# Edge convolution from split operands in a fused two-layer image and text kernel, with the unit order of the first layer rewritten

## What is computed

```python
gray = einsum('bchw,c->bhw', x, (0.2989, 0.587, 0.114))
edges = conv2d(gray, scharr, padding='SAME')       # 2 output channels, 3x3
edge = sqrt(edges ** 2).sum(axis=1) / 2            # |e0| + |e1|, halved
h = concat([edge, text_embedding(x_txt)], axis=1)  # 8 x 384 x 256
h = h + attn0(layernorm(h)); h = h + ternary_ffn(layernorm(h))
h = h + attn1(layernorm(h)); h = h + moe(layernorm(h))
```

## Time and profile before

| | us |
|---|---|
| median of 3 runs | 1999.88 |
| lowest and highest run | 1999.59, 2004.97 |
| profiled execution, its own time | 1996.78 |
| span of the profiled execution | 1995.0 |

### The profile page before, as it was taken

One profiled execution on the slowest core, in us unless ns is written; L12 is line 12 of the kernel. 1 busy time (PEld: TensorE's weight loads), 2 busy tenths in 40 slices (PEclk: granted clock), 3 DMA queues, 4 the chain that ended last, 5 costly groups with the idle time before them and its releaser, 6 DMA issues.

```text
span 1995.0 us, 35526 instructions
## 1 busy us (share of the span) xinstructions
PE 1768.5 (89%) x10970; PEld 1408.1 (71%) x10970; DVE 1237.8 (62%) x4024; ACT 957.3 (48%) x2645; POOL 552.9 (28%) x784
## 2 busy tenths in 40 slices
PE   3457999999999899899999999992499999999997
PEld 2244676767677686667777777771389998999896
DVE  7446686767777676756677776657754454445442
ACT  2025474666657566565666666640033343333331
POOL 2233324242423411211111111001333335434431
PEclk9668999999999999999999999995589999999998
DMA  6100101101010100102100110002212222222210
GB/s 193 56 27 17 51 2 58 35 24 56 3 43 0 56 26 8 33 1 58 33 32 32 32 32 0 24 25 81 73 48 98 81 75 66 77 72 67 61 38 20
DMA packets 74577, 90.44 MB, mean 45 GB/s; under 512 B 16539, under 2 KB 64710, under 8 KB 74472
## 3 DMA queue, kind: packets, MB, share of 16 engines
q1 hardware_dynamic: 65000, 72.49, 11.1%
q0 software_dynamic: 9472, 16.77, 3.0%
HBM read 71.26 MB, written 25.26 MB: 48 GB/s over the span
## 4 chain that ended last, share of the span: by engine, by line
PE 71%; issue 11%; DVE 8%; POOL 3%; ACT 2%; DVEq 2%; DMA 1%; POOLq 1%; SPq 1%; ACTq 0%
PE bank L1035 17%; PE bank L1539 16%; PE bank L1554 9%; PE bank L983 6%; PE bank L967 5%; PE bank L1018 5%; PE bank L1177 2%; PE bank L906 2%; PE bank L994 1%; PE bank L1057 1%; DVE probs L2177 1%; PE bank L891 1%; DVE at_least L2735 1%; PE bank L907 1%; POOL rstd_a L2946 1%
## 5 line engine op out<-in xcount | busy, mean ns | idle before, releaser
L1660 ACT ACTIVATE probs<-probs,nmax 128x128 f32<-128x128 f32 (+2 forms) x768 | 381.0, 501 | 75.3 <-DVE nmax L2177 75.1
L983 PE MATMUL bank<-cst,probs 128*128 128x128 f32 x1536 | 234.5, 279 | 19.4 <-ACT probsT L1668 11.6
L983 PEld LDWEIGHTS bank<-cst,probs 128*128 128x128 f32 x1536 | 182.4, 143 | 68.4 <-issue 25.8
L1539 PE MATMUL bank<-xeT,gate_w 128*128 128x480 f32 x768 | 189.3, 382 | 1.4 <-issue 1.4
L1539 PE MATMUL bank<-xeT,up_w 128*128 128x480 f32 x768 | 188.2, 380 | 0.0
L2272 DVE COPY probsT<-bank 128x384 f32<-128x384 f32 x256 | 141.4, 552 | 74.0 <-PE bank L983 72.4
L1554 PE MATMUL bank<-down_w,hT 128*120 128x256 f32 x1536 | 182.8, 281 | 0.0
L1554 PEld LDWEIGHTS bank<-down_w,hT 128*120 128x120 f32 x1536 | 181.5, 182 | 0.1
L2988 POOL COPY rinv<-rowsum 128x384 f32<-128x384 f32 x80 | 40.7, 509 | 497.3 <-DVE o1T L2199 294.5
L2882 DVE TENSOR_TENSOR prod<-bank,sil 128x480 f32<-128x480 f32 x128 | 83.8, 657 | 150.5 <-PE bank L1539 150.3
L1668 ACT COPY probsT<-bank 128x384 f32<-128x384 f32 x256 | 121.8, 476 | 113.1 <-PE bank L983 104.4
(11 more groups left out here) (314 smaller groups left out, 3325.1 us busy)
## 6 DMA issues: line engine op xcount, KB each, us to landing
gate_raw<-in_L_ffn_gate_w SPq DMA_DIRECT2D x8, 1024.0 KB, 4.8
up_raw<-in_L_ffn_up_w SPq DMA_DIRECT2D x8, 1024.0 KB, 6.9
down_raw<-in_L_ffn_down_w SPq DMA_DIRECT2D x8, 1024.0 KB, 5.7
img<-in_x SPq DMA_DIRECT2D x8, 768.0 KB, 5.1
residual_rows<-x SPq DMA_DIRECT2D x8, 384.0 KB, 2.5
residual_rows<-h_in SPq DMA_DIRECT2D x8, 384.0 KB, 3.8
xr<-residual_rows SPq DMA_DIRECT2D x8, 384.0 KB, 4.8
hr<-residual_rows SPq DMA_DIRECT2D x8, 384.0 KB, 3.7
```

Source lines behind the costliest of these rows:

```text
L983: last = tr(ps[bank][:, P * q:P * (q + 1)], probs[:, n % 4, SEG[t] + P * j:SEG[t] + P * (j + 1)], ident)
L1539: last = mm(ps[bank][:, 0:HALF], w[:, wp, c, P * m:P * (m + 1)], xeT[:, xp, c, HALF * hf:HALF * (hf + 1)], start=(c == 0 and k == 0), stop ...
L1660: last = f(p, p, ACT.Exp, bias=nmax[:, n % 4, t:t + 1], scale=-1.0, accum_out=rowsum[:, where, t:t + 1])
```

## The change

The filter bands and the gray image are each split into an upper part in the format F32R and a lower part, the rest. For each filter k the bank `conv{k}` now holds both image halves (512 columns), and nine F32R products (three shifts, times upper band with upper gray, upper band with lower gray, lower band with upper gray) and one halo product of 18 rows fill it. The upper gray part is made on ACT (`gray_uppers`), the lower one on DVE (`gray_lowers`); the halo goes by six transfers, each with three overlapping windows of 256 columns, into 18 rows, and ACT puts them into F32R, once for each half with a factor of 1 or 0 for each row (`halo_halves`). ACT writes the first filter's absolute values straight into `h_in` and the second's back into PSUM, and DVE adds them. The setup gets the splits of the weights and four more small loads ahead of `shift_c`.

```diff
...
+gray_hi, gray_lo = gray_parts[:, 0], gray_parts[:, 1]
...
@@ -413,15 +422,16 @@
...
-band = sb("band", [P, 2, 3, P])
-edge_w = sb("edge_w", [3, 2, 2, P])
+band_start = offsets["top"]
+band = sb("band", [P, 2, 2, 3, P], F32R)
+(band_f,), _ = region(band_start + 4 * 6 * P, ("band_f", [P, 2, 3, P], F32))
+edge_w = sb("edge_w", [18, 2, P], F32R)
...
@@ -636,11 +651,15 @@
     def load_halo(i):
-        sp.wait_ge(gray_ready, i + 1)
-        for k, row in enumerate((P - 1, 0)):
-            for dx in range(3):
-                sp.dma_start(halo_gray[dx:dx + 1, k, :], gray[row:row + 1, k, dx:dx + IMG]) \
-                    .then_inc(halo_loaded, 16)
+        sp.wait_ge(gray_split, i + 1)
+        if i > 0:
+            sp.wait_ge(halo_ready, i)
+        for hf, row in enumerate((0, P - 1)):
+            for part in range(3):
+                q = 9 * hf + 3 * part
+                src = gray_parts[row:row + 1, part % 2, 1 - hf, 0:IMG].bitcast(F32)
+                windows = bass.AP(src.tensor, src.offset, [src.ap[0], [1, 3], [1, IMG]])
+                sp.dma_start(halo_rows[q:q + 3, :], windows).then_inc(halo_loaded, 16)
     for s in range(2):
         sp.dma_start(tok[:, s, 1:], a["x_txt"]).then_inc(tokens_loaded, 16)
@@ -656,9 +675,9 @@
         (scharr_b[:].rearrange("p k a b -> p (k a b)"),
          a["L0_tok_scharr"].rearrange("k o a b -> (k o a b)").partition_broadcast(P)),
         (txt_scale, a["L0_txt_scale"].partition_broadcast(P)),
-        (scharr_h[:, 0, :], a["L0_tok_scharr"][0, 0].rearrange("a b -> b a")),
-        (scharr_h[:, 1, :], a["L0_tok_scharr"][1, 0].rearrange("a b -> b a")),
-        (shift_c[:], const[:, COLS["shift"][0]:COLS["shift"][1]]),
+        *[(scharr_h[3 * q:3 * q + 3, 0, :],
+           a["L0_tok_scharr"][:, 0, 2 - q // 3 * 2, :].rearrange("k b -> b k")) for q in range(6)],
+        (shift_c[:], const[:, COLS["shift"][0]:COLS["halo"][1]]),
         (wqkv[:], a["L0_attn_Wqkv"].rearrange("(c p) n -> p c n", p=P)),
         (w1[:], a["L0_attn_W1"].rearrange("(c p) n -> p c n", p=P)),
         (w2[:], a["L0_attn_W2"].rearrange("(m p) n -> p m n", p=P)),
@@ -798,12 +817,12 @@
             load_second()
             load_x()
             load_text_rows()
+            load_image_ahead()
+            load_residual()
             load_halo_rows()
-            load_residual()
-            load_image_ahead()
             spill_x()
+            spill_h()
             store_rows()
-            spill_h()
         else:
             load_x()
             load_residual()
@@ -892,20 +911,19 @@
                 if t == NT - 1:
                     last.then_inc(filled[bank], 1)
-    def convolve(sec, i, img_no, halves):
-        pe.wait_ge(gray_ready, at(img_no, 1, 1))
-        pe.wait_ge(halo_loaded, at(img_no, 96, 96))
-        for hf in halves:
-            name = f"conv{hf}"
+    def convolve(sec, i, img_no, kinds):
+        pe.wait_ge(gray_split, at(img_no, 1, 1))
+        pe.wait_ge(halo_ready, at(img_no, 1, 1))
+        for k in kinds:
+            name = f"conv{k}"
             bank = banks.bank(sec, name)
             banks.wait_free(pe, sec, name, i)
-            for k in range(2):
-                o = ps[bank][:, IMG * k:IMG * (k + 1)]
-                for dx in range(3):
-                    mm(o, band[:, k, dx, :], gray[:, hf, dx:dx + IMG], start=(dx == 0), stop=False)
-                last = mm(o, edge_w[:, hf, k, :], halo_gray[:, 1 - hf, :], start=False, stop=True)
-            last.then_inc(filled[bank], 1)
+            for dx in range(3):
+                for w, x in ((0, gray_hi), (0, gray_lo), (1, gray_hi)):
+                    mm(ps[bank][:], band[:, w, k, dx, :], x[:, :, dx:dx + IMG],
+                       start=(dx == 0 and w == 0 and x is gray_hi), stop=False)
+            mm(ps[bank][:], edge_w[:, k, :], halo[:], start=False, stop=True).then_inc(filled[bank], 1)
     pe.wait_ge(first_loaded, 16 * FIRST_LOADS)
@@ -1631,14 +1649,28 @@
         nc.scalar.copy(q0T[:, 4 * hh:4 * hh + 4, P * t:P * (t + 1)],
                        ps[bank][:].rearrange("p (q n) -> p q n", q=4)).then_inc(freed[bank], 1)
-    def edges(sec, i, img_no, hf):
-        banks.wait_filled(act, sec, f"conv{hf}", i)
-        if img_no[0] is not None or img_no[1] > 0:
-            act.wait_ge(var_ready[LN_FIRST], at(img_no, NT, hf - NT + 1))
-        f(edge[:, hf, :], ps[banks.bank(sec, f"conv{hf}")][:], ACT.Abs) \
-            .then_inc(freed[banks.bank(sec, f"conv{hf}")], 1)
+    def halo_halves(img_no):
+        act.wait_ge(halo_loaded, at(img_no, 16 * HALO_LOADS, 16 * HALO_LOADS))
+        for hf in range(2):
+            last = f(halo[:, hf, :], halo_rows[:], ACT.Identity, bias=0.0, scale=halo_side[:, hf:hf + 1])
+        last.then_inc(halo_ready, 1)
+    def gray_uppers(img_no):
+        act.wait_ge(gray_ready, at(img_no, 1, 1))
+        nc.scalar.copy(gray_hi[:, :, 1:IMG + 1], gray[:, :, 1:IMG + 1]).then_inc(gray_upper, 1)
+    def edges(sec, i, img_no, kinds=range(2)):
+        for k in kinds:
+            banks.wait_filled(act, sec, f"conv{k}", i)
+            bank = banks.bank(sec, f"conv{k}")
+            if k == 0:
+                if img_no[0] is not None or img_no[1] > 0:
+                    act.wait_ge(spilled, at(img_no, 32, 0))
+                f(h_in[:, 0:2, :].rearrange("p t d -> p (t d)"), ps[bank][:], ACT.Abs).then_inc(freed[bank], 1)
+            else:
+                f(ps[bank][:], ps[bank][:], ACT.Abs).then_inc(edge_ready, 1)
     def divisors_of(sec, i, name, layer, u, c):
         act.wait_ge(freed[5], out_index(layer, u, c, take0[5]))
@@ -1872,11 +1914,13 @@
             relu_of(6)
             relu_of(7)
-    for hf in range(2):
-        edges(SETUP, 0, (None, 0), hf)
+    gray_uppers((None, 0))
+    halo_halves((None, 0))
+    edges(SETUP, 0, (None, 0))
     ln_affine(PRO, 0, "lnA0", xTa[:, 0, :], 0, 2)
-    for hf in range(2):
-        edges(PRO, 0, (None, 1), hf)
+    gray_uppers((None, 1))
+    halo_halves((None, 1))
+    edges(PRO, 0, (None, 1))
     for hh in range(2):
         stack_upper_half((None, 0), hh, PRO, 0)
         for t in range(NT):
@@ -2060,19 +2105,33 @@
     ts(scharr_b[:], scharr_b[:], 0.5, None, ALU.mult)
     then()
-    shift = shift_c[:].rearrange("p (y m) -> p y m", y=3)
+    shift = shift_c[:, 0:3 * P].rearrange("p (y m) -> p y m", y=3)
     for y_ in range(3):
         for k in range(2):
             for dx in range(3):
                 w = scharr_b[:, k, y_, dx:dx + 1]
                 if y_ == 0:
-                    ts(band[:, k, dx, :], shift[:, 0, :], w, None, ALU.mult)
+                    ts(band_f[:, k, dx, :], shift[:, 0, :], w, None, ALU.mult)
                 else:
-                    stt(band[:, k, dx, :], shift[:, y_, :], w, band[:, k, dx, :], ALU.mult, ALU.add)
+                    stt(band_f[:, k, dx, :], shift[:, y_, :], w, band_f[:, k, dx, :], ALU.mult, ALU.add)
         then()
-    for k in range(2):
-        ts(edge_w[:, 0, k, P - 1:P], scharr_h[:, k, 2:3], 0.5, None, ALU.mult)
-        ts(edge_w[:, 1, k, 0:1], scharr_h[:, k, 0:1], 0.5, None, ALU.mult)
+    v.tensor_copy(band[:, 0], band_f[:])
+    halo_c = shift_c[0:18, 3 * P:3 * P + 3]
+    ts(scharr_h[:, 1, :], scharr_h[:, 0, :], 0.5, None, ALU.mult)
+    then()
+    v.tensor_copy(edge_hi[:], scharr_h[:, 1, :])
+    tt(band[:, 1], band_f[:], band[:, 0].bitcast(F32), ALU.subtract)
+    then()
+    stt(scharr_h[:, 2, :], edge_hi[:].bitcast(F32), halo_c[:, 2:3], scharr_h[:, 1, :], ALU.mult, ALU.add)
+    then()
+    v.tensor_copy(halo_side, halo_c[:, 0:2])
+    ts(edge_f[:, :, P - 1], scharr_h[:, 2, :], halo_c[:, 0:1], None, ALU.mult)
+    ts(edge_f[:, :, 0], scharr_h[:, 2, :], halo_c[:, 1:2], None, ALU.mult)
+    then()
+    v.tensor_copy(edge_w[:], edge_f[:])
+    sides = slice(0, IMG + 2, IMG + 1)
+    for z in (gray_hi, gray_lo):
+        v.tensor_copy(z[:, :, sides], small[:, 34:36].unsqueeze(1).to_broadcast([P, 2, 2]))
@@ -2119,26 +2178,33 @@
         else:
             ts(dst, k[:, 0:S], cols[:, g:g + 1], cols[:, b:b + 1], ALU.mult, ALU.add).then_inc(f_, 1)
-    def edges(sec, i, img_no, hf):
-        banks.wait_taken(dve, sec, f"conv{hf}", i)
-        if img_no[0] is not None or img_no[1] > 0:
-            dve.wait_ge(spilled, at(img_no, 32, 0))
-        tt(h_in[:, hf, :], edge[:, hf, 0:IMG], edge[:, hf, IMG:2 * IMG], ALU.add)
+    def edges(sec, i, img_no, halves=range(2)):
+        dve.wait_ge(edge_ready, at(img_no, 1, 1))
+        k, f_ = bank_of(sec, "conv1", i)
+        for hf in halves:
+            last = tt(h_in[:, hf, :], h_in[:, hf, :], k[:, IMG * hf:IMG * (hf + 1)], ALU.add)
+        if 1 in halves:
+            last.then_inc(f_, 1)
     def gray_image(c):
         dve.wait_ge(img_loaded, at(c, 16, 16))
         if c[0] is not None or c[1] > 0:
-            dve.wait_ge(halo_loaded, at(c, 96, 0))
+            dve.wait_ge(halo_loaded, at(c, 16 * HALO_LOADS, 0))
         inner = gray[:, :, 1:IMG + 1]
         ts(inner, img[:, 0], GRAY[0], None, ALU.mult)
         then()
```

(13 more changed lines are left out.)

389 lines of the change are left out of this document (207 added, 182 removed).

## The result

The changed kernel took 2051.62 us (median of 4 runs, 2042.91 to 2053.28) against 2000.91 for the kernel before on the same chip (4 runs): 1.024 times as long, 95% interval 1.0208 to 1.0274. It is slower by 2.4%, where I had forecast 1987.0, faster. The profiled execution took 2053.28 us with a span of 2051.4, 56.4 more than before.

The account below looks back on a forecast made before the run. TensorE's own work was taken to bound units 1 to 5, and dependence chains unit 0. Terms -13 (iterations), -5.5 (unit 0), -1 (units 6 and 7), +7 (setup, prologue) gave -12.5 from 1999.88: 1987 us, range 1972 to 1999.

Parts of the forecast that it names:

- The products: Convolution on TensorE: 20 F32R products of 512 columns at 0.254 to 0.302 us each, saving 3.2 us an image.
- the fourth rival: F32R convolution products stream at full rate, 0.215 us each; six units gain 0.8 us each, 1982.6 in all; chance 0.05.
- The start of an iteration: Loop's turn: `divisors_last` waits 1.7 us instead of 2.81, gaining 1.1; a new wait of 1.5 follows at `values(1)`.
- The same gap of DVE stands at each of the loop's turns, so I take it as belonging to the turn, and it stays.: Turn of the first loop: DVE's idle 3.02 us before `invert_last` remains after the change.
- The wait for the divisors' copy: Start of an iteration: TensorE waits 1.5 us at `values(1)`, since ACT's gray copy precedes its copy of the divisors.
- I find no wait in the following part: Iteration up to `norm_mlp`, by DVE's and ACT's lists: no further wait after the 0.2 us at `values(2)` and `queries_keys(0)`.
- What the other engines get: ACT gets 1.3 us more on 54.9, DVE a lower part of 0.74; both lie under TensorE's 81 us of work.
- The prediction had -2.6: One iteration of the first loop: 3.2 + 1.1 - 1.5 - 0.2 = 2.6 us gained, five iterations 13.
- Setup and prologue: Ahead of the first stack products: setup +3.2 us (1 to 6), prologue +3.8, both together +7.
- Unit 0: First unit: POOL's third rotation 5 us earlier and 0.5 from elsewhere, -5.5 us, between 0 and -10.
- Units 6 and 7: Units with changed lists and unchanged work: part of a wait ahead of `norm_mlp` goes, -1 us, from +2 to -4.
- The signs that it had named: Forecast wrong if TensorE waits ahead of the halo product, convolution instructions exceed 0.3 us, or the prologue costs over 10.

Follow-up runs that it names:

- the pair of runs in one order: Changed kernel, third attention normalization moved back, VectorE loops not refetched each turn: new convolution (gray copy behind divisors' copy) 1986.2 us; old convolution and setup 1996.97.
- The placed kernel before: Kernel before with empty VectorE instructions at the head, so that neither VectorE loop is transferred anew at each turn: 1989.5 us.
- only the code is placed: Changed kernel with nothing but 67 empty instructions at VectorE's head, so that neither loop is transferred anew at each turn: 2009.02 us, ratio 1.0039.
- the two placed kernels: Kernel before (1989.5 us) and changed kernel with normalization back and gray copy behind divisors' copy (1986.2), both with VectorE loops not transferred anew each turn.
- the gray image later: Against the changed kernel repaired and placed: VectorE's gray image behind its first value rows, ScalarE's gray copy behind its third exponential group: 1997.09 us, ratio 0.9969.
- repaired and placed: Changed kernel, third attention normalization moved back, gray copy behind divisors' copy, VectorE loops shifted so neither is transferred anew each turn: 1986.2 us, ratio 0.9915.
- 1985.4: Changed kernel, third attention normalization moved back, 67 empty VectorE instructions so neither loop is refetched each turn, gray copy still ahead of divisors' copy: 1985.41 us, ratio 0.9918.
- 51 together: Changed kernel with normalization moved back, gray copy behind divisors' copy and 110 empty VectorE instructions: 2000.24 us, ratio 0.9985; alone 2019.1, 2037.2, 2035.5.

## Why the prediction was wrong

**The products: right.** Forecast 3.2 us less an image, 2.9 by the trace (5.47 for 8.3) and 2.94 by the pair of runs in one order. Nine products of 512 columns in 2.37 us are 0.263 each, inside the range that I took from the rows of 256 and 384 columns; the fourth rival, 0.215, did not come. (The section that it was taken from, the Trainium skill, TensorE: Matmul & The Clock Gate, Back-to-back issue gap, gives this rule for a single product by itself, and for a sustained stream of products of 512 columns a lower figure, 131 ns; the F32R products here took 0.263 us, more than either.)

**The start of an iteration: the step that failed is "The same gap of DVE stands at each of the loop's turns, so I take it as belonging to the turn, and it stays."** It belongs to where VectorE's code lies. The placed kernel before has no such wait and is 11.5 us faster. In the changed kernel the gap was 3.58 instead of 3.02, TensorE waited 2.18 us where 1.7 was forecast, and the clock fell at these waits, which I had not priced at all: of the 95.6 us of an iteration 7.0 go when only the code is placed (88.6). In the kernel before, where the clock held, the gap cost 88.6 - 85.6 = 3.0. The wait for the divisors' copy, 1.5 forecast and 1.16 measured, was right, and most of it belonged to the same cause (0.49 is left when only the code is placed).

**"I find no wait in the following part": wrong.** The added lists were right for what DVE and ACT do and left out POOL. At the end of the iteration stood 2.81 us of wait and 1.6 to 3.4 of lost clock; 4.4 in sum where it stands by itself. The step "What the other engines get" did not ask what POOL does at that time, though `attn_norm(2)` was moved in the diff and releases it. The Trainium skill, SBUF — State Buffer, section Who interferes with whom, says that a VectorE instruction with two SBUF inputs, or a cast in a two-port mode, waits for the whole length of a GpSimd instruction that holds the pair of ports they share. The trace agrees: 1.95 and 1.96 us beside additions of 1.83 and 2.12, each ending 0.2 to 0.4 us behind the addition that it overlaps. It agrees in what was not slowed too: in the kernel before the first of the same additions lay beside masks and a copy that read from PSUM, and these kept their 0.55 us. The kernel before had one normalization of 1.92 us beside another of POOL's additions, so that the trace at hand could have given the warning.

**The second layer: not in the prediction.** +17.3 us by 18 instructions of displacement, more than the prediction's whole sum of -12.5. That all eight units and everything after them could move with a static position was no term and no rival.

**An iteration, put together** from the runs: -2.94 products, +1.6 the order, +4.4 POOL beside DVE, +4.0 the turn (7.0 for 3.0) = +7.1, and the trace has 95.6 - 88.6 = +7.0. The prediction had -2.6. Each term is the difference of two runs in a chain from the kernel before to the changed one, so that the sum must come out; that it does is no proof of the terms. What each stands for rests on the waits and stretches in those runs.

**Setup and prologue: right in the sum, not in the parts.** +7 forecast, +8.9 measured up to the first stack product; between the two placed kernels it is 6.2 (125.95 and 119.73). Start-up differs by up to 6 us among runs of one convolution (113.73, 115.14 and 120.17 with the old one), so that the agreement proves little. The setup cost 1.6 us where 3.2 was forecast (ACT's last absolute value ends at 78.65 for 77.01): its products start 6.8 us later, where 6.3 was forecast, but take 6.95 us and not 8.6. The prologue cost 7.3 where 3.8 was forecast: its products start at 110.16 for 106.4 (1.6 of this comes from the setup) and take 9.3, above the 5.1 to 8.6 of the forecast. At the low clock, twice 5.1 = 10.2, as the prediction itself has it for the setup, was the right bound. Its mean clock of 0.61 for the setup's products is that of 61 to 75 us, which begins before them; over the products themselves it was 0.69.

**Unit 0: mechanism right, result wrong.** POOL's last rotation comes 51.2 us after the first stack product instead of 55.4, 4.2 earlier where 5 was forecast, but the unit ends 2.5 later instead of 5.5 earlier. With 64 us at half clock it took 102.2 and 102.3 in two of the experiments, with 76 to 79 us 106.3 to 106.7 in the changed kernel and six of the experiments, with 86 us 109.9 in one (the gray image later), and before the change 103.9. What brings the clock down there I did not separate.

**Units 6 and 7:** -2.8, forecast -1.

**The signs that it had named did not come.** TensorE did not wait for the halo, a product took 0.26 us in the loop and not over 0.3, and setup and prologue together cost less than 10. All three looked at the convolution, and the loss lay in what stands around it.

**What stays open:** whether the change, repaired and placed, beats the kernel before placed as well. The ratios of 1986.2 and 1985.4 and that of 1989.5 have overlapping intervals. Side by side on one chip, four runs of 1984.64 to 1987.53 stand against five of 1987.19 to 1990.78: 3.3 us less by the medians, 0.2%, which speaks for a small gain and does not settle it. The loop gains 8.1 us in the profiled executions (420.8 for 428.8), and setup and prologue take 6.2 back. What decides whether the clock falls at a wait, and for how long, is open too. Why the new order's transposes are busy for 1.3 us more was not tried.

## What to carry to other kernels

Before a change to the length of a program with loops is priced, look at the queue of instruction transfers and at idle time put down to "issue" at each turn: if a loop shows them, try the same kernel with a few dozen empty instructions at its head before anything else, and compare two versions only when their loops are both kept. A step that is moved on one engine releases work on another, and VectorE and GpSimd can hold each other up; ask which instruction will run beside it, and look in the trace of before for one that is several times longer than others of its shape. A wait of 2 to 3 us on TensorE cost its length here, or up to 3.4 us more, and repairs of such waits did not add up (63 us apart, 51 together).
